# A two-layer transformer kernel: the experts' second product partly in bf16 halves, merged loads first, and small score blocks of layer 1 packed into shared banks

## The reference

```
x = x + ga * attention0(norm(x))     # 16 heads of 8, relative positions
x = x + gb * experts0(norm(x))       # 2 shared experts + 8 routed ones, top 2 kept by weights
x = x + ga * attention1(norm(x))     # 16 score heads of 8, causal, two softmaxes subtracted
x = x + gb * expert1(norm(x))        # one expert with relu, layer norm
```

```
h = gelu(xf @ W1[e] + b1[e])   # 128 -> 512, erf gelu
y = h @ W2[e] + b2[e]          # 512 -> 128
moe = sum_e w[t, e] * y[e]     # w is zero outside the top two
```

## Time and profile before

| what | value |
|---|---|
| median of 3 runs | 2532.14 us (2531.35 to 2536.93) |
| the profiled execution's own time | 2532.68 us |
| its span, first to last instruction | 2530.9 us |
| TensorE busy | 2171.6 us, 86% |
| VectorE busy | 1642.4 us, 65% |
| ScalarE busy | 1332.3 us, 53% |
| GpSimd busy | 707.1 us, 28% |
| mean granted TensorE clock | 0.933 |

### The profile page before, as it was taken

How to read it: one execution, slowest core, us unless ns; L and a number is a source line. 1 busy time by engine, 2 the same in 40 slices (tenths; PEclk the granted TensorE clock), 3 DMA queues, 4 the chain that set the end, 5 groups by cost and what they waited for, 6 DMA issues and landing times. The chain is left out here.

```text
span 2530.9 us, 50478 instructions
## 1 busy us (share of the span) xinstructions
PE 2171.6 (86%) x16122; PEld 1283.9 (51%) x16250; DVE 1642.4 (65%) x3386; ACT 1332.3 (53%) x2282; POOL 707.1 (28%) x573
## 2 busy tenths in 40 slices
PE   3663999999999999999849998999997498899586
PEld 1331677777777777777624444444443244444232
DVE  3885788888888888888634343443433688888354
ACT  1220566666666666666525445545453155555454
POOL 1443544444444444444102221222123000000000
PEclk9775999999999999999969999999998699999799
DMA  4443111111111111111020212202211222222221
GB/s 172 138 149 120 36 41 39 39 39 39 39 39 39 42 39 40 40 41 37 17 83 21 71 63 92 87 33 80 74 67 51 67 81 81 87 83 71 88 79 42
DMA packets 94927, 163.61 MB, mean 65 GB/s; under 512 B 18120, under 2 KB 44242, under 8 KB 93586
## 3 DMA queue, kind: packets, MB, share of 16 engines
q1 hardware_dynamic: 94866, 162.82, 20.4%
HBM read 102.37 MB, written 60.41 MB: 64 GB/s over the span
## 5 line engine op out<-in xcount | busy, mean ns | idle before, releaser
L1131 ACT ACTIVATE prob<-prob,neg_max_h 128x640 f32<-128x640 f32 x512 | 425.5, 831 | 325.4 <-DVE neg_max_h L1031 324.8
L1031 DVE CUSTOM_DVE_ANT_0 prob<-pair,pair_mask 128x640 f32<-128x640 f32 x512 | 419.1, 819 | 137.5 <-PE pair L948 136.3
L1607 PE MATMUL pair<-hid,down_w 128*128 128x512 f32 x640 | 309.6, 630 | 30.2 <-DVE moe L1392 25.0
L1910 ACT ACTIVATE prob_h<-pair 128x256 f32<-128x256 f32 (+3 forms) x512 | 205.7, 436 | 193.5 <-PE pair L1797 186.8
L1094 POOL TENSOR_TENSOR a_full<-rot_c,rot_s 128x512 f32<-128x512 f32 x128 | 163.2, 1275 | 500.5 <-DVE rot_s L1018 500.5
L1038 DVE TENSOR_TENSOR prob<-prob 128x128 f32<-128x128 f32 x512 | 272.5, 532 | 0.5 <-ACT prob L1131 0.5
L1533 ACT ACTIVATE hid<-pair,up_b 128x512 f32<-128x512 f32 x320 | 200.8, 691 | 128.7 <-PE pair L1587 128.4
L1849 DVE TENSOR_REDUCE row_max<-pair 128x1 f32<-128x128 f32 (+3 forms) x512 | 221.3, 485 | 54.8 <-PE pair L1776 50.3
L904 PE MATMUL outsum<-ident,prob 128*128 128x128 f32 x1024 | 249.7, 275 | 3.9 <-ACT prob_t L1139 0.5
L904 PE MATMUL turn<-ident,prob 128*128 128x128 f32 x1024 | 250.4, 275 | 0.1
L1607 PEld LDWEIGHTS pair<-hid,down_w 128*128 128x128 f32 x640 | 125.8, 201 | 188.6 <-issue 159.8
(11 more groups left out here) (268 smaller groups left out, 4453.8 us busy)
## 6 DMA issues: line engine op xcount, KB each, us to landing
vx_d<-vx SPq DMA_DIRECT2D x16, 1024.0 KB, 4.8
o_d<-out_sb SPq DMA_DIRECT2D x64, 256.0 KB, 2.0
w_all<-w_d SPq DMA_DIRECT2D x8, 2048.0 KB, 7.2
val<-vx_d SPq DMA_DIRECT2D x32, 256.0 KB, 6.6
val_h<-vx_d SPq DMA_DIRECT2D x32, 256.0 KB
qs_d<-part_q SPq DMA_DIRECT2D x48, 128.0 KB
ks_d<-part_k SPq DMA_DIRECT2D x48, 128.0 KB
num<-o_d SPq DMA_DIRECT2D x24, 256.0 KB
```

The lines of the kernel that those rows point to most:

```text
L1031: nc.vector.tensor_tensor_reduce(prob[s % 4][:, :], pair[:, cols], pair_mask[:, cols], -1.0, 3.0e38, ALU.add, ALU.min, neg_max[par][:, s:s ...
L1131: nc.scalar.activation(prob[s % 4][:, :], prob[s % 4][:, :], ACT.Exp, bias=neg_max[par][:, s:s + 1], scale=-1.0).then_inc(exp_done.sem, 1)
L1607: mm = nc.tensor.matmul(out_ap, down_w[:, EXPERTS[i], c, :], hid[i % 2][:, c, :], start=(c == 0 and i != 1), stop=(c == HC - 1 and i != 0))
L1910: nc.scalar.activation(prob_h1[jb % 2][:, h, jb * P:S], bank[u % EXP_BANKS][:, jb * P:S], ACT.Exp, scale=SCALE).then_inc(h1_exp_used.sem, 1)
```

## The change

Six edits. (1) Of each expert's four chunks of `hid`, chunks 2 and 3 are multiplied in `down` as three bf16 products each (`HB` = 2); chunks 0 and 1 stay fp32 (`HF` = 2). (2) For that ScalarE applies gelu to chunks 2 and 3 a second time, from the same bank, into bf16 `hid_hi`; VectorE computes `hid_lo` = `hid` - `hid_hi` in a new `split_hidden`. (3) GpSimd splits half of `W2` in the projection stage. (4) SyncE issues `loads(ahead)` before `spread_weights(b)`. (5) VectorE does `shared(b)` before `merge(ahead)`. (6) In layer 1 blocks of several heads that fit one bank of 512 columns share it: one mask matmul for all of them, one reduction, one exp. The copies of the sums and of the turned maxima move from VectorE to ScalarE, and the negation into the reduction.

```diff
     def split_weights(e, count):
+        for i, (hi_e, lo_e, whole_e) in enumerate((up_parts, down_parts)):
+            ones = ones_col[:, :].broadcast_to([P, (HID, HB * D)[i]])
+            nc.gpsimd.tensor_tensor(hi_e, whole_e, ones, ALU.mult).then_inc(weight_parts.sem, 1)
+            g.wait_ge(weight_parts.sem, weight_parts.at(4 * count + 2 * i + 1))
+            nc.gpsimd.tensor_tensor(lo_e, whole_e, hi_e, ALU.subtract).then_inc(weight_parts.sem, 1)
...
     def both(b, ahead, behind):      # SyncE
+        if ahead is not None:
+            loads(ahead)
         spread_weights(b)
         if ahead is not None:
-            loads(ahead)
+            load_mod0(ahead)
...
+    def split_hidden(b, i):          # VectorE
+        v.wait_ge(down_done.sem, down_done.at(NX * b + i - 1))
+        for c in range(HB):
+            v.wait_ge(gelu_done.sem, gelu_done.at(NX * HC * b + HC * i + HF + c + 1))
+            v.wait_ge(gelu_hi_done.sem, gelu_hi_done.at(NX * HB * b + HB * i + c + 1))
+            ve.tensor_tensor(hid_lo[i % 2][:, c, :], hid[i % 2][:, HF + c, :], hid_hi[i % 2][:, c, :],
+                             ALU.subtract).then_inc(hid_lo_done.sem, 1)
...
     def both(b, ahead, behind):      # VectorE
+        split_hidden(b, 0)
         if behind is not None:
             ln1.center(v, "d", behind, x2, f3_pe, f3_dve)
+        split_hidden(b, 1)
+        shared(b)
         if ahead is not None:
             merge(ahead)
-        shared(b)
         for i in range(NSH, NX):
+            split_hidden(b, i)
...
     def gelu(b, i):                  # ScalarE, after the fp32 gelu of chunk c
+            if c >= HF:
+                nc.scalar.activation(hid_hi[i % 2][:, c - HF, :], bank[c][:, :], ACT.Gelu,
+                                     bias=up_b[:, EXPERTS[i], c:c + 1]).then_inc(gelu_hi_done.sem, 1)
...
     def up(b, i):                    # TensorE
+            if c >= HF:
+                pe.wait_ge(gelu_hi_done.sem, gelu_hi_done.at(NX * HB * b + HB * (i - 1) + c - HF + 1))
...
     def down(b, i):                  # TensorE
-        for c in range(HC):
+        for c in range(HF):
             pe.wait_ge(gelu_done.sem, gelu_done.at(HC * e + c + 1))
-            mm = nc.tensor.matmul(out_ap, down_w[:, EXPERTS[i], c, :], hid[i % 2][:, c, :],
+            nc.tensor.matmul(out_ap, down_f[:, EXPERTS[i], c, :], hid[i % 2][:, c, :],
...
+        for c in range(HB):
+            pe.wait_ge(hid_lo_done.sem, hid_lo_done.at(HB * e + c + 1))
+            nc.tensor.matmul(out_ap, w_hi, hi, start=False, stop=False)
+            nc.tensor.matmul(out_ap, w_lo, hi, start=False, stop=False)
+            mm = nc.tensor.matmul(out_ap, w_hi, lo, start=False, stop=(c == HB - 1 and i != 0))
...
+    MAX_ITEMS = [(0, 0, 4), (1, 0, 2), (1, 2, 2)] + [(ib, h, 1) for ib in (2, 3) for h in range(GH)]
+    EXP_ITEMS = [(jb, h, 1) for jb in (0, 1) for h in range(GH)] + [(2, 0, 2), (2, 2, 2), (3, 0, 4)]
...
     def max_item(n, k, r, m):        # TensorE; exp_item alike
+        nc.tensor.matmul(dst[:, :, i0:w], identb[:, :], mask_low.unsqueeze(1).broadcast_to([P, heads, P]),
+                         start=True, stop=False, skip_group_check=True)
+        for x in range(heads):
+            mm = nc.tensor.matmul(dst[:, x, :], q_h1[k][0:KM, h0 + x, i0:w], k_h1[k][0:KM, h0 + x, 0:w],
+                                  start=False, stop=(x == heads - 1), skip_group_check=True)
...
     def group(g, k, r, first=False): # TensorE
+        for s in range(NU):
             if ahead is not None:
+                for _ in range(min(2 if s < 4 else 1, NM - m)):
+                    max_item(*ahead, m)
                     m += 1
+            exp_item(g, k, s)
             if s == 1 and not first:
                 values(g - 1, (k - 1) % H1_BUFS, NB - 1)
+            for jb in range(NB - 1):
+                if s == UP_TO[jb] + (1 if jb < 2 else 0):
+                    values(g, k, jb)
+            if s == 9 and ahead is not None:
                 turn_maxima(ahead[0])
...
+    def group(g, k, first=False, last=False):   # ScalarE
+        for u in range(NU):
+            exp_item(g, k, u)
+            if u == 2 and not first:
+                sums(g - 1)          # copy of out_bank, waits for values(3) of group g-1
+            if u == NU - 2 and not last:
+                negated(g + 1)       # copy of bank 6, waits for the turn
```

More of the change, by code:

```diff
@@ L50 @@
 HC = HID // P
+HF = 2
+HB = HC - HF
 NE = 8
@@ L641, in split_weights @@
             def split_weights(e, count):
-                ones = ones_col[:, :].broadcast_to([P, HID])
                 at = slice(e, e + 1) if isinstance(e, int) else bass.ds(e, 1)
[L645 to L648, removed]
+                up_parts = [x[:, at].rearrange("p e n -> p (e n)") for x in (up_hi, up_lo, up_w)]
+                down_parts = [x[:, at].rearrange("p e c d -> p (e c d)") for x in (down_hi, down_lo, down_w)]
+                for i, (hi_e, lo_e, whole_e) in enumerate((up_parts, down_parts)):
[3 more added lines that the diff above has]
+                    nc.gpsimd.tensor_tensor(lo_e, whole_e, hi_e, ALU.subtract).then_inc(weight_parts.sem, 1)
             g.wait_ge(load_ffn, 16 * len(ffn_loads))
@@ L1187, in build @@
         hid = [fsb(f"hid{i}", [P, HC, S]) for i in range(2)]
+        hid_hi = [fsb(f"hid_hi{i}", [P, HB, S], BF16) for i in range(2)]
+        hid_lo = [fsb(f"hid_lo{i}", [P, HB, S], BF16) for i in range(2)]
         term = [fsb(f"term{i}", [P, S]) for i in range(2)]
@@ L1843, in h1_v, with row_maxima @@
             ve = nc.vector
[L1845 to L1850, removed]
+            def row_maxima(n, k):
+                for m, (ib, h0, heads) in enumerate(MAX_ITEMS):
+                    w = (ib + 1) * P
+                    v.wait_ge(h1_max_ready.sem, h1_max_ready.at(NM * n + m + 1))
+                    src = bank[EXP_BANKS + (NM * k + m) % MAX_BANKS][:, 0:heads * w].rearrange("p (h n) -> p h n", h=heads)
+                    ve.tensor_reduce(row_max1[:, h0:h0 + heads, ib], src, AX_X, ALU.max, negate=True
+                                     ).then_inc(h1_max_used.sem, 1)
@@ L1870, in group @@
-            def group(g, k, r, first=False):
+            def group(g, k, r):
                 ahead = following(g, k, r)
                 if ahead is not None:
[L1873 to L1878, removed]
+                    row_maxima(ahead[0], ahead[1])
                     negatives(ahead[0], ahead[1])
@@ L1889, in h1_v @@
                                    identb[KM:KM + GH, KM + h:KM + h + 1].broadcast_to([GH, S])).then_inc(h1_init, 1)
-            for h in range(GH):
-                row_maxima(0, h)
+            row_maxima(0, 0)
             negatives(0, 0)
             for k in range(H1_BUFS):
-                group(k, k, 0, first=(k == 0))
+                group(k, k, 0)
             with v.Fori(1, NG // H1_BUFS - 1) as r:
@@ L1900, in h1_v, with h1_a, exp_item, sums @@
                 group(H1_BUFS * r + k, k, r)
-            sums(NG - 1)
[L1903 to L1911, removed]
+        def h1_a(act):
+            def exp_item(g, k, u):
+                jb, h0, heads = EXP_ITEMS[u]
+                w = S - jb * P
+                if h0 == 0:
+                    act.wait_ge(h1_pv_done.sem, h1_pv_done.at(NB * g + jb - 1))
+                act.wait_ge(h1_exp_ready.sem, h1_exp_ready.at(NU * g + u + 1))
+                nc.scalar.activation(prob_h1[jb % 2][:, h0:h0 + heads, jb * P:S],
+                                     bank[(NU * k + u) % EXP_BANKS][:, 0:heads * w].rearrange("p (h n) -> p h n", h=heads),
+                                     ACT.Exp, scale=SCALE).then_inc(h1_exp_used.sem, 1)
+            def sums(g):
+                act.wait_ge(h1_pv_done.sem, h1_pv_done.at(NB * (g + 1)))
+                act.wait_ge(h1_stored.sem, h1_stored.at(16 * g))
+                nc.scalar.copy(out_sb1[:, :], out_bank[:, :]).then_inc(h1_copied.sem, 1)
+            def negated(n):
+                act.wait_ge(h1_turned.sem, h1_turned.at(n + 1))
+                act.wait_ge(h1_neg_max.sem, h1_neg_max.at(n))
+                nc.scalar.copy(neg_max1[KM:KM + GH, :], bank[6][KM:KM + GH, :]).then_inc(h1_negated.sem, 1)
+            def group(g, k, first=False, last=False):
[5 more added lines that the diff above has]
+                        negated(g + 1)
+            negated(0)
+            for k in range(H1_BUFS):
+                group(k, k, first=(k == 0))
+            with act.Fori(1, NG // H1_BUFS - 1) as r:
+                for k in range(H1_BUFS):
+                    group(H1_BUFS * r + k, k)
+            for k in range(H1_BUFS):
+                group(NG - H1_BUFS + k, k, last=(k == H1_BUFS - 1))
+            sums(NG - 1)
```

78 lines of the change are left out of this document (37 added, 41 removed).

## The result

| | before | after |
|---|---|---|
| median | 2532.51 us (2531.35 to 2536.93, 4 runs) | 2491.43 us (2489.95 to 2496.84, 4 runs) |
| span of the profiled execution | 2530.9 us | 2488.2 us |
| ratio of the times, 95% interval | | 0.9839 (0.9819 to 0.9858) |

A forecast was written before the change was run, and what follows sets the result against it. TensorE was taken as fullest in the expert stage and layer 1, with VectorE's program order a second bound inside a batch; VectorE fullest in projection. 2532.7 + 5 - 13 - 32 = 2493 us, forecast range 2475 to 2512, whole range 2458 to 2533.

The forecast's parts named there:

- Expert stage: -13 forecast: Expert stage: seven batches at -1.3 us each give -9, the last batch -3.5; bounds -68 and +48.
- (a): Batch stretch from the first `up` to `project_q`: 31.2 us, forecast -5.2, to 26.0.
- (b): Batch stretch from `project_q` to `mean_c`: 14.7 us, VectorE sets the time, forecast +1.8, to 16.5.
- (c): Batch stretch from `mean_c` to the router's result: 24.8 us, forecast +1.5.
- (d): Batch stretch from the router's result to the next batch: 9.2 us, forecast +0.6.
- The stall's price: Expert stage: TensorE idle 3.2 us a batch for `moe` behind `merge`'s DMA wait, then 1.8 at the lower clock; both go.
- Layer 1: -32 forecast: Layer 1's heads: group of 10.99 us becomes 9.2 + 0.3 + 0.5 = 10.0, saving 1.0 in 31 groups.
- Projection: +5 forecast: Projection stage: GpSimd's two extra operations per batch hold VectorE 0.6 us, 8 batches, +5 (0 to +9).
- (1) The whole 34 us come off: Rival, expert stage: VectorE and ScalarE keep up, all 34 us and the stalls come off, 2437; chance 0.10.
- (2) Layer 1 gains only 2 to 5: Rival, layer 1: two-bank alternation of exps replaces the stalls, 2 to 5 us left of the 32, 2520; chance 0.22.
- (3) Loads no sooner: Rival, expert stage: loads land at 20.5 us as now, `down(2)` waits 3 us a batch, 2514; chance 0.10.
- (4) Slower by held subtractions: Rival, expert stage: VectorE bounds it, pairs held by GpSimd's sum, lower clock, +5 per batch, 2542; chance 0.08.

The follow-up runs named there:

- e1: Kernel before with only the layer 1 edit, nothing of the expert or projection stage: 2510.94 us, ratio to before 0.9929.
- e2: Changed kernel without the bf16 halves (second product stays fp32; new order of loads and shared sum, new layer 1): 2470.73 us, ratio to before 0.9768.
- e4: Changed kernel with ScalarE's copy of the sums in layer 1 ahead of exp 2 instead of behind it: 2485.03 us, ratio to before 0.9822.
- e7: e2 with the copy of the sums ahead of exp 2 and `values(0)` behind exp block 6 instead of 5: 2458.72 us, ratio to before 0.9722.
- e10: e7 with bf16 halves for experts 0, 1 and 2 of the order alone and `values(0)` behind exp block 7: 2446.33 us, ratio to before 0.9667.
- e3: Changed kernel with the old order of loads and shared sum (bf16 halves and new layer 1 kept): 2527.27 us, ratio to before 0.9988.
- e9: Changed kernel with GpSimd's sum of the experts cut to one of its 512 columns: 2472.02 us, ratio to before 0.9761.
- e5: Changed kernel without VectorE's `split_hidden` subtractions, `hid_hi` taking the place of `hid_lo` in the third product: 2465.58 us, ratio to before 0.975.
- e6: Changed kernel without ScalarE's second gelus, `hid_hi` a constant, subtractions kept: 2473.75 us, ratio to before 0.9785.

## Why the prediction was right in the sum and wrong in its terms

**Expert stage: -13 forecast, -25.4 measured.** The stretches of a batch came as forecast: (a) 26.3 against 26.0, (b) 16.1 against 16.5, (c) 25.8 against 26.3, (d) 9.7 against 9.8, together 77.9 against 78.6. The waits named for them are there; the 0.4 ahead of `project_out` was not named, and of the 2.9 at `up` 8 a wait of 1.5 start to start stood there before. What failed more is the base. I took one batch of 79.9 us for all. The starts of `h_lo` in the trace of before, and in that of after (one line of the kernel, first and last start):

```profile
L1386 DVE TENSOR_TENSOR h_lo<-ht,h_hi x8: 693/1641/1642, 1308.9 to 1867.1; 128x512 bf16<-128x512 f32 x8
```
```profile
L1402 DVE TENSOR_TENSOR h_lo<-ht,h_hi x8: 691/1637/1639, 1313.9 to 1851.6; 128x512 bf16<-128x512 f32 x8
```

In before the six steady intervals are 80.4, 81.0, 81.6, 79.8, 80.9, 81.6: I had the shortest. In after all six are 77.9. So a steady batch saved 3.0, not 1.3: 1.0 by the base, 0.7 by the stretches. Seven intervals gave 558.2 - 537.7 = 20.5 against 9; the last batch 4.8 against 3.5.

Nor is all of the 25.4 the change's. e1 has the expert code of before, and its stage takes 700.4 us where that of before takes 708.2:

```profile
L1386 DVE TENSOR_TENSOR h_lo<-ht,h_hi x8: 692/1638/1640, 1310.8 to 1861.7; 128x512 bf16<-128x512 f32 x8
```

Its six batches are 78.2 to 81.2 and average 80.0, which is my base. Against e1 the change saves 17.6 us in the stage and 2.1 a batch, so some 8 of the 12.4 that I missed are the difference between two executions of the same code; the 0.7 by the stretches stays. In the three traces with the old order, where `merge` waits for its loads, the six batches of a trace lie 1.8 to 3.0 us apart, in the changed kernel 0.03: of the old order neither one batch nor one execution is a measure.

**The parts of that stage.** The forecast held that the order removes 5.0 a batch and the halves give 3.7 back. The runs: 5.5 (80.0 to 74.5) and 3.4 (74.5 to 77.9). The halves' 0.42 per expert is real (4.2 us a batch less of matmuls) and is not paid out, because each needs 1.2 us of ScalarE and 1.3 to 2.4 of VectorE in program order. The stall's price, 3.2 and 1.8 by the clock together, is borne out to half a microsecond by both pairs of runs, 5.5 with fp32 and 4.8 with the halves; no run parts the two.

**Layer 1: -32 forecast, -20.8 measured.** The two waits that the change brings were forecast at 0.3 and 0.5 and are 0.29 and 0.53. The step that failed is "TensorE's own work is about 9.2 us". I had measured the stalls of before from the last matmul that the chain names, and TensorE had more matmuls behind it. TensorE ahead of the second of them:

```profile
2157.96 0.22 PE L1776 MATMUL pair<-masks,identb 128*128 128x128 bf16 x1
2158.01 0.27 PE L1774 MATMUL pair<-k_h,q_h 96*128 96x256 bf16 x1
2158.13 0.22 PE L1776 MATMUL pair<-masks,identb 128*128 128x128 bf16 x1
2158.68 0.22 PE L1797 MATMUL pair<-masks,identb 128*128 128x128 bf16 x1 [0.33 <-ACT prob_h L1910]
```

It works until 2158.18, so 0.50 is lost, not 0.7; likewise 0.87, not 1.0, at the turn. That leaves 10.99 - 1.37 = 9.6 us of work and small gaps (0.10 ahead of each `values`), and 9.6 + 0.8 = 10.4 is the group measured. So a group saves 0.59 of the 10.99, 0.65 of the average of 11.05, where I forecast 1.0.

**Projection: +5 forecast, +4.4 measured**, about where it was put: VectorE's `ln_normed` went from 1185 to 1386 ns on average (13 in the stage), `xn` from 627 to 912 (7): 2.6 + 2.0. In the other traces with all the halves the stage takes 202.9 to 209.6 us, in those without 198.0 to 200.6, so only the sign and the rough size are sure.

**The rivals.** (1) The whole 34 us come off: refuted by e2, which is faster without the halves. (2) Layer 1 gains only 2 to 5: no, though its mechanism, exps in order over two banks, is what e4, e7 and e10 gained 0.5 a group from. (3) Loads no sooner: no; e3, where they come no sooner, waits 3.6 us for `moe` in a batch, and its batches are 82.7. (4) Slower by held subtractions: the holding is real (e9: up to 3.4 a batch), but the 5.5 of the new order outweigh it.

## What to carry to other kernels

Read the period of a loop from all its rounds and from more than one execution, and a stall from where the last matmul has streamed its columns to the next start; here the base, 1.0 us off in 80 for this trace, was off by nearly the gain forecast from it, 1.3. When an edit buys matmul time with work on other engines, count where in their program order that work falls: halves for three experts of ten, at places where ScalarE and VectorE have room, gain 6.7 us, a fourth loses 7.4. Edits of one change can work against each other: together they gain 41, and without the halves the kernel is another 18 to 21 us faster.

## What the runs showed of the hardware

GpSimd's sum of 512 columns stretches a VectorE subtraction beside it from 0.69 to 1.64 us. With the sum cut short a batch takes 74.5 us, as long as with fp32; with the whole sum it takes 77.9; how much of that is the stretching stays open. The Trainium skill (SBUF — State Buffer, section Who interferes with whom) says that a VectorE instruction with two SBUF inputs contends with a GpSimd instruction that reads SBUF; the 0.69 and 1.64 agree.

A lower clock is not always a loss. Behind the router the granted clock falls in some batches of the changed kernel (0.76 over 7 us) and not in others (1.00), and its batches last 77.9 us either way, the second kind with a wait of 1.5 us for `term` at the same place. My expectations for e5 and e6 counted 1.8 us for it. In e5 that wait came in its place, in e6 the lower clock stayed (0.60 from 1600 to 1603), so neither gained it.

A mask matmul of 256 columns in two runs of 128 takes 0.12 us to the next start (2146.26 to 2146.38), one of 128 columns in one run 0.06 (2145.51 to 2145.57): the same rate. So the Trainium skill's warning (PSUM — Partial Sum Buffer, section Specifications) of non-contiguous patterns, which I had priced at 14 us, is not borne out for runs of this length; the measurement decides.
